# Gated linear attention inside a twelve-layer kernel: query norms on token-major rows, scores in 64x64 blocks, merged factor products, contexts copied by ScalarE

## The reference, cut to what matters

```
h = _rmsnorm(x, g_attn)
q = _l2norm((h @ Wq).reshape(B, T, N_HEADS, D_K))
k = _l2norm((h @ Wk).reshape(B, T, N_HEADS, D_K))
v = (h @ Wv).reshape(B, T, N_HEADS, D_V)
alpha = jax.nn.sigmoid(h @ Wg).reshape(B, T, N_HEADS, D_K)
def step(S, inp):
    a_t, k_t, v_t, q_t = inp
    S = a_t[..., None] * S + k_t[..., None] * v_t[..., None, :]
    o_t = jnp.einsum('bhkv,bhk->bhv', S, q_t)
    return (S, o_t)
...
return o @ Wo
```

## Time and profile before

| | |
|---|---|
| three executions | 2826.84, 2822.14, 2827.99 us (median 2826.84) |
| the profiled execution | span 2826.2 us from the first to the last instruction |
| PE, PEld busy over the span | 2198.0 us (78%), 1519.0 us (54%) |
| DVE, ACT, POOL busy over the span | 1816.6 us (64%), 1290.3 us (46%), 1179.0 us (42%) |
| the gated linear attention | from about 34 us to 869 us of the span |

### The profile page before, as it was taken

The page is one execution under the profiler, slowest core; times in us unless marked ns, Lnnn a source line. Parts: engine busy times, 40 slices in busy tenths (PEclk is TensorE's granted clock), DMA queues, the critical chain, the costliest instruction groups (busy, mean ns, idle before and its releaser), DMA issues. The chain is left out here.

```text
span 2826.2 us, 46612 instructions
## 1 busy us (share of the span) xinstructions
PE 2198.0 (78%) x15104; PEld 1519.0 (54%) x15104; DVE 1816.6 (64%) x4918; ACT 1290.3 (46%) x2801; POOL 1179.0 (42%) x1150
## 2 busy tenths in 40 slices
PE   2799999999998679329479997959999999952780
PEld 0466666666666557317345554845566666541560
DVE  3677777687775767301367774649888888857113
ACT  1445454544543227313335564736666666620223
POOL 1424233342421100545422221558777787710663
PEclk9899999999999759569779997969999999965885
DMA  6400000000002000012333332000000000000113
GB/s 197 104 1 0 0 0 0 0 0 0 0 0 68 0 0 0 31 54 67 89 90 90 85 83 79 0 1 1 0 0 0 0 0 0 0 30 0 43 42 94
DMA packets 103412, 88.55 MB, mean 31 GB/s; under 512 B 12060, under 2 KB 90166, under 8 KB 103222
## 3 DMA queue, kind: packets, MB, share of 16 engines
q1 hardware_dynamic: 96150, 72.67, 9.5%
q0 software_dynamic: 7168, 14.73, 1.7%
HBM read 59.02 MB, written 40.96 MB: 35 GB/s over the span
## 5 line engine op out<-in xcount | busy, mean ns | idle before, releaser
L3278 POOL TENSOR_SCALAR mb_w<-mb_duT,mb_bT 128x256 f32<-128x256 f32 x512 | 468.0, 933 | 118.0 <-PE bank L3288 81.6
L3213 DVE TENSOR_TENSOR_SCAN mb_hs<-mb_dA,bank 128x512 f32<-128x512 f32 x256 | 300.9, 1205 | 35.9 <-issue 25.0
L38 POOL TENSOR_TENSOR scrap<-ones 128x1 f32<-128x1 f32 x64 | 12.5, 195 | 695.9 <-DVE gla_ss L421 488.6
L3307 PE MATMUL bank<-mb_hc,ident 128*128 128x512 f32 x512 | 257.7, 627 | 15.6 <-DVE mb_hc L3223 15.3
L3269 ACT ACTIVATE mb_dA<-mb_delta,mb_A 128x255 f32<-128x255 f32 x512 | 216.6, 495 | 9.2 <-DVE mb_hs L3213 9.1
L2435 DVE TENSOR_REDUCE ra_mx<-bank 128x2 f32<-128x512 f32 x256 | 163.9, 686 | 61.3 <-PE bank L2289 58.7
L2017 ACT ACTIVATE e_hid<-bank,e_b 128x512 f32<-128x512 f32 (+1 forms) x128 | 79.6, 634 | 258.5 <-PE bank L2061 191.4
L2525 ACT ACTIVATE ra_pT<-bank 128x512 f32<-128x512 f32 x256 | 141.2, 600 | 114.3 <-PE bank L2311 114.0
L3288 PE MATMUL bank<-ident,mb_w 128*128 128x128 f32 x1024 | 149.9, 280 | 34.3 <-DVE mb_hs L3213 26.3
L3223 DVE TENSOR_TENSOR mb_hc<-mb_hs,bank 128x1024 f32<-128x1024 f32 x128 | 153.0, 1195 | 0.0
L2096 DVE TENSOR_TENSOR e_y<-bank,e_b 128x512 f32<-128x512 f32 (+1 forms) x32 | 20.0, 625 | 197.8 <-PE bank L2071 120.2
(11 more groups left out here) (552 smaller groups left out, 5917.1 us busy)
## 6 DMA issues: line engine op xcount, KB each, us to landing
results<-const_empty SPq DMA_DIRECT2D x2, 4096.0 KB
e_got<-results SPq DMA_DIRECT2D x32, 256.0 KB, 3.3
rope_rows<-ra_part SPq DMA_DIRECT2D x48, 128.0 KB, 1.9
ra_k<-rope_rows SPq DMA_DIRECT2D x32, 192.0 KB, 3.3
ra_q<-rope_rows SPq DMA_DIRECT2D x32, 192.0 KB, 4.3
queue<-const_spare_rows SPq DMA_DIRECT2D x1, 4128.0 KB
e_x<-queue SPq DMA_DIRECT2D x8, 516.0 KB
e_w<-in_L_ffn_w SPq DMA_DIRECT2D x2, 2048.0 KB, 8.2
```

Of the source, the lines that this page charges most:

```text
L3213: dve.tensor_tensor_scan(hs[n // 2 % 2][:, n % 2, :, :].rearrange("p c t -> p (c t)"), dA[n % RD][:, :, :].rearrange("p c t -> p (c t)"), ...
L3278: ins = pool.tensor_scalar(w[n % RH][:, h, :], duT[k][:, h, :], bT[k][:, h, n:n + 1], None, ALU.mult)
L3307: ins = pe.matmul(YB[:, :], g.ident[:, :], hc[grp % 2][:, j, :, :].rearrange("p c t -> p (c t)"), start=(n == 0), stop=(n == NS - 1))
```

## The change

Five things change, all in `gla`.

1. Query norms. The split, the transposes (L357), `sel` (L496) and DVE's multiplication (L551) go. POOL multiplies the query rows in token-major form by their norms, in place, in two instructions (4 heads, then 12 heads of 64 channels for both tiles), ahead of the transposes. ACT copies the contexts from PSUM into `oT`, which has two buffers now.
2. Scores. Each full 128x128 product within a tile becomes two 64x64 blocks on the diagonal, so eight matmuls of 64 rows, 64 weight columns and 64 columns in place of four with 128 and 128; the quarter that is never seen is not computed. The product between tiles comes first. The two heads' banks are one array, and DVE copies 768 elements in one instruction.
3. Factors. Queries and keys lie side by side: one product of 512 elements from PSUM and two of 256 in SBUF in place of two of 256 and four of 128.
4. Gates. ACT takes |z| from PSUM in place of DVE's L416; Exp follows, and Ln after z3.
5. Order. In a step PE runs project, all items, scores, context. The items come in the order y h | k0 k1 k2 | k3 q0 q1 | q2 q3 | z0 z1 | z2 z3 | v0 v1 | v2 v3; y is that of three sequences earlier (`LAG`). `sq` has two buffers. POOL's order in a turn is key norms, query norms, scaled queries, log gates.

```diff
-    PLAN = {0: ("", "", "h"), 1: ("z0", "z1", "z2"), 2: ("y", "z3", "k0"), 3: ("k1", "k2", "k3"),
-            4: ("q0", "q1", "q2"), 5: ("q3", "v0", "v1"), 6: ("v2", "", "v3"), 7: ("", "", "r")}
+    PLAN = {0: ("y", "h"), 1: ("k0", "k1", "k2"), 2: ("k3", "q0", "q1"), 3: ("q2", "q3"), 4: ("z0", "z1"), 5: ("z2", "z3"),
+            6: ("v0", "v1"), 7: ("v2", "v3")}
+    LAG = 3
...
     def pe_project(pe, s, k, hp):
         if hp == 0:
             pe.wait_ge(ktok_ready, s * 4 + 4)
-            pe.wait_ge(qtok_ready, s * 4 + 4)
+            pe.wait_ge(qs_ready, s * 2 + 1)
+        if hp == 2:
+            pe.wait_ge(qs_ready, s * 2 + 2)
...
     def pe_scores(pe, s, hp):
+        for hd, r in enumerate(HALVES):
+            pe.matmul(SC[:, hd, 2 * P:3 * P], f128[b][r, 0, :], f128[b][r, 1, :], start=True, stop=True)
+        for t in range(2):
+            for part in HALVES:
+                for hd, r in enumerate(HALVES):
+                    pe.matmul(SC[part, hd, t * P + part.start:t * P + part.stop], km[r, t, part], qm[r, t, part],
+                              start=True, stop=True)
         for t in range(2):
             for hd, r in enumerate(HALVES):
-                pe.matmul(SC[hd][:, t * P:(t + 1) * P], km[b][r, t, :], qm[b][r, t, :], start=True, stop=True)
-        for hd, r in enumerate(HALVES):
-            pe.matmul(SC[hd][:, 2 * P:3 * P], k128[b][r, :], q128[b][r, :], start=True, stop=True)
...
     def pe_context(pe, s, k, hp):
-        pe.matmul(OB[:, 256:512], sel[:, 2 * hp:2 * hp + 2, :].rearrange("p h d -> p (h d)"), rqT[k][:, :],
-                  start=True, stop=True)
...
+    def act_context(act, s, k, hp):
+        act.wait_ge(o_psum, at(s, hp))
+        act.activation(oT[k][:, hp, :], context_bank(hp), ACT.Copy).then_inc(o_ready, 1)
...
     def dve_factors(dve, s, hp):
+        dve.tensor_tensor(mid[b][:, 0:4 * P].rearrange("p (j t c) -> p j t c", j=KQ, t=2),
+                          QK[:, :].rearrange("p (j t c) -> p j t c", j=KQ, t=2), ex[b][:, :, :, 0:P],
+                          ALU.mult).then_inc(mid_ready, 1)
+        dve.wait_ge(mid_ready, at(s, hp))
+        dve.tensor_tensor(f64[b][:, :, :, :], early_k_late_q,
+                          edge[:, :, 0:2].rearrange("p t j -> p j t").unsqueeze(3).broadcast_to([P, KQ, 2, 64]), ALU.mult)
+        dve.tensor_tensor(f128[b][:, :, :].rearrange("p j (h c) -> p j h c", h=2), first_k_second_q,
+                          edge[:, :, 2:4].unsqueeze(3).broadcast_to([P, KQ, 2, 64]), ALU.mult).then_inc(qkx_ready, 1)
...
     def dve_seen(dve, s, hp):
+        dve.copy_predicated(sT[b][:, :, :], g.seen[:, :].unsqueeze(1).broadcast_to([P, 2, 3 * P]), SC)\
+            .then_inc(sc_ready, 1)
...
+            def scaled_queries(s, k):
+                pool.wait_ge(rnq_ready, s + 1)
+                for heads in (slice(0, 4), slice(4, HEADS)):
+                    n = heads.stop - heads.start
+                    rows = tok["q"][k][:, :, heads.start * DK:heads.stop * DK].rearrange("p t (h d) -> p t h d", d=DK)
+                    pool.tensor_tensor(rows, rows, rnq[:, :, heads].unsqueeze(3).broadcast_to([P, 2, n, DK]), ALU.mult)\
+                        .then_inc(qs_ready, 1)
...
             with pool.Fori(0, NSEQ // 2) as i:
                 for k in R:
-                    scales(i * 2 + k, 1, rnk[:, :, :], kss_ready, kmax_ready, rnk_ready)
-                    log_gates(i * 2 + k, k)
-                    scales(i * 2 + k, 0, rnq[:, :, :], qss_ready, qmax_ready, rnq_ready)
-                    parts(i * 2 + k)
+                    scales(i * 2 + k, 1, rnk[:, :, :], rnk_ready)
+                    scales(i * 2 + k, 0, rnq[:, :, :], rnq_ready)
+                    scaled_queries(i * 2 + k, k)
+                    log_gates(i * 2 + k, k)
```

More of the change, by code:

```diff
@@ L352, in pe_item @@
         elif kind == "y":
[L353 to L358, removed]
+            pe_result(pe, s - LAG, 1 - k, PB)
         else:
-            if item == "z0":
+            if item == "k0":
                 pe.wait_ge(h_ready, s + 1)
@@ L378, in act_item @@
     def act_item(act, s, k, item):
-        if not item:
-            return
         PB = bank_of(item)
-        kind, c = item[0], int(item[1:] or 0)
+        kind, c = kind_of(item)
         if kind == "h":
@@ L582, in start_of @@
-    def start_of(item, tokens=None):
-        def start(eng, step):
-            if step == 0 and tokens:
-                tokens(eng, 0)
-            for x in PLAN[step]:
-                item(eng, 0, 0, x)
-        return start
-    def end_of(one_back, two_back, result):
-        def end(eng):
-            s = NSEQ - 1
-            one_back(eng, s, 1, HP - 1)
-            two_back(eng, s, 1, HP - 2)
-            two_back(eng, s, 1, HP - 1)
-            if result:
-                result(eng, s)
-        return end
@@ L600, in none, with nothing, in_steps @@
-    def none(*args):
-        pass
+        dve.copy_predicated(sT[b][:, :, :], g.seen[:, :].unsqueeze(1).broadcast_to([P, 2, 3 * P]), SC)\
+            .then_inc(sc_ready, 1)
+    def nothing(*args):
+        pass
+    def in_steps(eng, body, end):
+        for step in range(HP):
+            body(eng, None, 1, 0, step)
+        for s in range(LAG):
+            for step in range(HP):
+                body(eng, s, s % 2, s + 1, step)
+        with eng.Fori(0, (NSEQ - 1 - LAG) // 2) as i:
+            for j in range(2):
+                for step in range(HP):
+                    body(eng, i * 2 + (LAG + j), (LAG + j) % 2, i * 2 + (LAG + j + 1), step)
+        for step in range(HP):
+            body(eng, NSEQ - 1, 1, NSEQ, step)
+        end(eng)
@@ new lines, in over, with back, items_of, result_of @@
+    def over(s, step, n):
+        return s is not None and (step >= n or not first(s))
+    def back(s, k, step, n):
+        return (s, k, step - n) if step >= n else (s - 1, 1 - k, HP + step - n)
+    def items_of(nxt, step):
+        if isinstance(nxt, int) and nxt == NSEQ:
+            return {0: ("y",), 4: ("y",)}.get(step, ())
+        return PLAN[step]
+    def result_of(nxt, step):
+        return NSEQ + 1 if step and isinstance(nxt, int) and nxt == NSEQ else nxt
+    def pe_body(pe, s, k, nxt, step):
+        if s is not None:
+            pe_project(pe, s, k, step)
+        for item in items_of(nxt, step):
+            if isinstance(nxt, int) and nxt == NSEQ and step:
+                pe.wait_ge(y_ready, NSEQ - 2)
+                pe_result(pe, NSEQ - 2, k ^ 1, bank_of("y"))
+            else:
+                pe_item(pe, nxt, 1 - k, item)
+        if over(s, step, 1):
+            sb_, _, hb = back(s, k, step, 1)
+            pe_scores(pe, sb_, hb)
+        if over(s, step, 2):
+            pe_context(pe, *back(s, k, step, 2))
@@ new lines, in pe_end, with act_body @@
+    def pe_end(pe):
+        s = NSEQ - 1
+        pe_scores(pe, s, HP - 1)
+        pe_context(pe, s, 1, HP - 2)
+        pe_context(pe, s, 1, HP - 1)
+        pe.wait_ge(y_ready, s)
+        pe_result(pe, s, 1, bank_of("y"))
+    def act_body(act, s, k, nxt, step):
+        if s is not None:
+            act_exponentials(act, s, step)
+        for item in items_of(nxt, step):
+            act_item(act, nxt, 1 - k, item)
+        if over(s, step, 2):
+            act_context(act, *back(s, k, step, 2))
@@ new lines, in act_end, with dve_body @@
+    def act_end(act):
+        act_context(act, NSEQ - 1, 1, HP - 2)
+        act_context(act, NSEQ - 1, 1, HP - 1)
+    def dve_body(dve, s, k, nxt, step):
+        items = items_of(nxt, step)
+        if s is not None:
+            dve_factors(dve, s, step)
+        if step == 0 and not (isinstance(nxt, int) and nxt == NSEQ):
+            dve_tokens(dve, nxt)
+        for n, item in enumerate(items):
+            if n == 1 and over(s, step, 1):
+                sb_, _, hb = back(s, k, step, 1)
+                dve_seen(dve, sb_, hb)
+            if isinstance(nxt, int) and nxt == NSEQ and step:
+                dve_result(dve, NSEQ - 2, bank_of("y"))
+            else:
+                dve_item(dve, nxt, 1 - k, item)
+        if len(items) < 2 and over(s, step, 1):
+            sb_, _, hb = back(s, k, step, 1)
+            dve_seen(dve, sb_, hb)
```

264 lines of the change are left out of this document (93 added, 171 removed).

## The result

| | before | after |
|---|---|---|
| executions side by side | 2826.84, 2822.14, 2827.99, 2829.66 us | 2774.50, 2787.58, 2777.86, 2777.55 us |
| median | 2827.41 us | 2777.70 us |
| span of the profiled execution | 2826.2 us | 2772.7 us |

The ratio is 0.9833 (95% interval 0.9814 to 0.9852): 1.7% faster, about 50 us. The forecast was 2744 us. The time lies inside the wide range (2703 to 2795), but outside the forecast's own band (2730 to 2765) and 34 us above the forecast itself: of 82.5 us foreseen, 50 came.

The account below looks back on a forecast made before the run. PE was taken to bound the turn: 41.0 work + 1.8 + 1.3 waits = 44.1 us. Fifteen turns save 75, start 4, turn 1 3.5: 2826.8 - 82.5 = 2744 us; 2703 to 2795 holds 8 in 10.

Parts of the forecast that it names:

- PE's work, 41.0 us a turn: PE's own work in a turn of the new kernel, without waits: 41.0 us, 4.6 less than before.
- Waits of 1.8 + 1.3: PE's waits a turn: 1.8 us around scaled queries and Ln (steps 5, 6), 1.3 around log gates (steps 6, 7).
- The wait for Ln inside the other: PE's 1.4 us wait for exponentials behind Ln lies mostly inside the roughly 2 us hold from DVE's blocking; both together 1.8.
- 0, as long as PE is the later one: ACT's and DVE's changed work adds 0 us to the turn while PE is later; ACT gains 2.5, DVE stays near 31.
- Start, 4 us: At the layer's start, log gates are ready at 86 against log-gate sums at 90.5: 4 us less (bounds 0 and 8).
- Turn 1 has no y: 3.5 less: Turn 1 has no y to compute, so it takes 3.5 us less.
- The fifteen turns at 44.1: Each turn takes 41.0 + 1.8 + 1.3 = 44.1 us, 5.0 less; over fifteen turns 75 us.
- An unseen wait, 2780: Rival: the log-gate chain lacks its 1.5 us slack, or an unseen wait of 0.3 us opens every step: 2780; chance 0.12.
- Blocks one at a time: Rival: small blocks in the scores run singly or issue too slowly, 0.85 us in place of 0.27: 2806; chance 0.13.
- no blocking: Rival: POOL and DVE do not hold each other, so the turn is 42.4 us: 2719; chance 0.20.
- a slow multiplication on POOL: Rival: POOL's multiplication with a repeated norm is slow; at 8 ns an element the turn is 53.0 us: 2878; chance 0.07.

Follow-up runs that it names:

- Pieces: The changed kernel with POOL's scaled queries and log gates each issued as pieces of 512 elements, the loop kept: 2754.7 us (ratio 0.9757).
- full products, shifted: The changed kernel with four 128x128 products in place of the eight small blocks, and PE's loop 80 waiting instructions further on: 2771.6 us (ratio 0.9819).

## Why the prediction was right, and where it was not

PE's work and the waits between engines came out close to the forecast. The time landed 34 us above it for a reason that the working has no term for. That it still lies in the range is the range's width: the band it fell into (2765 to 2795) had 0.12, and for log gates that come late or a wait in every step, and neither was there.

- **PE's work, 41.0 us a turn: right.** 41.2 busy, each part within 0.04 us, the blocks four at once.
- **Waits of 1.8 + 1.3: right in size, partly in course.** DVE is held to the end of POOL's elementwise instruction, as foreseen, 2.98 and 3.02 us in place of 0.42. POOL's rows took 1.04 and 2.94 (1.2 and 3.4 foreseen). What I hadn't followed: z3's minimum stood behind the held product, so the log gates slid by 1.3 us and held the next product for 2.6 us and not 1.5. The 1.8 at v1 and behind Ln came as 0.8 and 0.4, the 1.3 at v3 as 2.0: the sum was right because two errors nearly cancelled.
- **The wait for Ln inside the other: right.** Pieces uncovered it as 1.5, near the 1.4 of the earlier trace rows, and moving Ln took it away.
- **Context copies, "0, as long as PE is the later one": wrong.** In every turn it was DVE that PE's waits ended with; giving the copies back to it costs 11 us. The forecast has no term for this. Whether its waits held the gain by chance is not shown.
- **Start, 4 us: right in size, in part by luck.** The second h came at 86.98, 4.4 earlier than before. The log-gate sums came at 82.27, 8.2 earlier than in the earlier trace rows and not 4; then PE waited 3.5 us for `gla_hn`, which the forecast does not have.
- **"Turn 1 has no y: 3.5 less": wrong.** Without y nothing covers DVE's normalising of the tokens, and PE waited 3.5 us for `gla_hn`, in turns 0 and 1. After the second wait the sums at 134.55 still took 1.09 us, the lower level, and that stretch 47.58. Together 6.7 us above the forecast.
- **The fifteen turns at 44.1: the step that failed.** The working added PE's work and its waits for data, and put what it costs to jump back, and the clock after an idle stretch, at nothing without a reason. By stretches, from h of turn 1 (86.98) to the last h (740.30) are 653.3 us; the forecast gives 14 x 44.1 - 3.5 = 613.9. The 39.4 between them are: five turns with the slow jump, 22.8 over the plain 44.45 (14.8 gap, 8.0 the clock's fall behind it, which the wait of 2.0 alone brings too, as the kernel with its loop written out shows); four others, 5.7, the clock's fall after the wait of 2.0; twelve times 0.35 for the plain turn, 4.2; and the 6.7 of the first two. So 29 of them are no instruction's time and no wait between engines. Nothing in my working asked how many instructions the loop has, or where it starts, though the change adds over two hundred to it. The whole section is 36.4 us over the forecast: start and end gave 1.4 back, and 1.7 is only that the old turns were a little longer than the 49.1 I took. The layers behind it, which were not changed, took 7 us less in this pair of profiled executions. Such a difference needs no cause in the change: from the layer's last matmul to the program's last the fourteen traces have 1875 to 1894 us.
- **Rivals.** "An unseen wait, 2780" named the right time for another reason. "Blocks one at a time" (2806) is excluded by 0.28, "no blocking" (2719) by the 2.98 and 3.02, and a slow multiplication on POOL (2878) by 2.94 us for 1536 elements, 1.9 ns each.

## What to carry to other kernels

When a change alters the number of instructions in a loop that the bounding engine runs, look for idle "issue" time at the first instruction of the body, and at the packets of the instruction queue. Packets alone do not show a stall: the loop written out fetched 92 and had no gap. Here the same loop was fast from one start and slow from another, and the slow jump cost 3 to 7 us a pass, while the small blocks saved 0.9 us a turn, 1.8 a pass. Write the loop out, or shift it, before judging the edit. POOL's elementwise multiplications and subtractions held DVE's products of two SBUF inputs until their end (3.0 us in place of 0.42), so long ones are better cut into pieces, and each wait taken away had the next one under it (v3, then Ln, then the log gates, then `gla_hn`). Follow them down until the engine that bounds is busy throughout.

## What the runs showed of the hardware

- PE's jump back took 0.21 to 0.24 us or 3.3 to 4.2 us, and for one and the same body by its place alone: 1664 instructions, 0.21 to 0.24 and, 128 further on, 3.6 to 4.2; 1622 instructions, 3.3 to 3.7 and, 80 further on, 0.21 to 0.24. When slow it fetched some nine blocks of 256 instructions (55 packets more in six jumps, 45 in five).
- After gaps of up to 3.2 us and waits of 2.0 and 3.5 us PE's granted clock went, in most turns but not in all, to its lower level for some us (sums 1.08 in place of 0.62). In the kernels without a gap, the last twelve turns up to the last h were all plain where the waits were 1.5 us at most. With 1.8 us (full products, shifted) all were but one, which took 46.97 in place of 45.45.
- In the same turn POOL's power of 5.46 us did not hold DVE's products back (0.42 at 431.64 beside it), its multiplications and subtractions did. The Trainium skill (SBUF — State Buffer, section "Who interferes with whom") says that a DVE instruction with two SBUF inputs contends with a POOL (GpSimd) instruction that reads SBUF; the trace agrees for the multiplications and subtractions and not for the power.
- Eight 64x64 fp32 blocks, 16 passes of 64 columns, took 0.28 us between them, where one pass of 64 columns takes 0.053 by the rate of the sums: four tiles at work at once.
